# Ten masks on ScalarE in every second head, and an earlier register read on TensorE

## What is computed

```python
for h in range(8):
    Wx = x @ Ws[h] + Wb[h]
    s = Wx[dst] @ a_w[h, :d] + Wx[src] @ a_w[h, d:] + a_b[h]
    s = leaky_relu(s, 0.2)
    alpha = segment_softmax(s, dst)
    out[h] = segment_sum(alpha * Wx[src], dst)
```

## Time and profile before

| | |
|---|---|
| Runs | 561.11, 562.78 and 562.98 us, median 562.78 |
| The profiled execution | 560.58 us, of which the span from its first to its last instruction is 558.8 |
| Start and tables | 0 to 21.5 us |
| Counting of edges | 21.5 to 147.8 us |
| Masks and weighted sums of the eight heads | 147.9 to 261.4 us |
| The rest | 261.4 to 558.8 us |
| Busy share of the span | PE 89%, DVE 85%, ACT 61%, POOL 12% |

### The profile page before, as it was taken

The page is one execution under the profiler, slowest core; times in us unless marked ns, Lnnn a source line. Parts: engine busy times, 40 slices in busy tenths (PEclk is TensorE's granted clock), DMA queues, the critical chain, the costliest instruction groups (busy, mean ns, idle before and its releaser), DMA issues.

```text
span 558.8 us, 12125 instructions
## 1 busy us (share of the span) xinstructions
PE 499.0 (89%) x4635; PEld 371.2 (66%) x4636; DVE 472.7 (85%) x933; ACT 342.7 (61%) x663; POOL 68.3 (12%) x83
## 2 busy tenths in 40 slices
PE   1879999887589999999889999998999999999995
PEld 1757777765488888889777754543456686877662
DVE  7899999799899999996898947997687686997771
ACT  5365555567889999997456452334444457865830
POOL 3000000000000000000000020122423520321232
PEclk9989999999989999999999989999999999999999
DMA  6980000002001111100000039100001017966111
GB/s 173 360 290 2 1 2 1 2 4 95 3 1 50 54 74 60 54 3 2 1 0 2 1 112 392 43 1 1 2 11 50 38 64 261 389 242 220 61 53 52
DMA packets 25306, 45.14 MB, mean 81 GB/s; under 512 B 6961, under 2 KB 7205, under 8 KB 25248
## 3 DMA queue, kind: packets, MB, share of 16 engines
q1 hardware_dynamic: 23264, 39.16, 20.4%
q0 software_dynamic: 1952, 5.18, 2.5%
q10 hardware_dynamic: 32, 0.01, 0.0%
HBM read 33.23 MB, written 11.95 MB: 81 GB/s over the span
## 4 chain that ended last, share of the span: by engine, by line
DVE 41%; PE 37%; issue 10%; DMA 5%; ACT 4%; POOL 3%; ACTq 0%; POOLq 0%; DVEq 0%
PE bank L1390 7%; PE bank L1414 5%; PE bank L1457 4%; DVE work L1082 4%; DVE big L950 4%; PE bank L1780 4%; PE bank L1464 4%; PE bank L1561 3%; PE bank L1574 2%; DMA aux<-xperm_scratch 2%; DVE st L849 2%; PE bank L1368 2%; POOL row L489 2%; DVE rings L1082 2%; DMA out<-aux 2%
## 5 line engine op out<-in xcount | busy, mean ns | idle before, releaser
L950 DVE TENSOR_TENSOR big<-mid 128x1536 f16<-128x1536 f16 (+1 forms) x100 | 92.1, 978 | 0.0
L1457 PE MATMUL bank<-big 128*128 128x160 f16 x552 | 72.2, 248 | 4.1 <-DVE big L950 4.1
L1561 PE MATMUL bank<-big,work 128*128 128x130 f16 x1080 | 67.2, 224 | 8.4 <-DVE work L1082 8.4
L1561 PEld LDWEIGHTS bank<-big,work 128*128 128x128 f16 x1080 | 64.0, 100 | 10.5 <-DVE work L1082 4.9
L1457 PEld LDWEIGHTS bank<-big 128*128 128x128 f16 x552 | 51.7, 111 | 6.7 <-DVE big L950 6.3
L657 ACT ACTIVATE mid<-aux,small 128x1280 f16<-128x1280 f32 x36 | 47.4, 1349 | 0.7 <-DVE work L1082 0.4
L1574 PE MATMUL bank<-big,mid 128*128 128x260 f16 x400 | 47.1, 275 | 0.1
L1656 PE MATMUL bank<-mid 128*128 128x512 f16 x200 | 47.2, 378 | 0.0
L556 ACT ACTIVATE big<-bank 128x160 f32 x92 | 27.9, 304 | 26.5 <-PE bank L1464 25.2
L556 ACT ACTIVATE mid<-bank 128x160 f32 x92 | 27.8, 303 | 25.8 <-PE bank L1464 24.4
L1574 PEld LDWEIGHTS bank<-big,mid 128*128 128x128 f16 x400 | 38.2, 96 | 7.5 <-issue 0.3
(11 more groups left out here) (313 smaller groups left out, 1123.4 us busy)
## 6 DMA issues: line engine op xcount, KB each, us to landing
big<-in_L_ffn_W SPq DMA_DIRECT2D x10, 1024.0 KB, 14.0
mid<-in_L_ffn_W SPq DMA_DIRECT2D x6, 1024.0 KB, 15.1
xperm_scratch<-work SPq DMA_DIRECT2D x1, 5753.0 KB, 20.2
aux<-thr_scratch SPq DMA_DIRECT2D x8, 640.0 KB, 3.8
aux<-xperm_scratch SPq DMA_DIRECT2D x8, 523.0 KB, 4.5
row<-in_x SPq DMA_DIRECT2D x1, 2304.0 KB
aux<-in_L_gnn_Ws SPq DMA_DIRECT2D x4, 256.0 KB, 4.5
work<-in_L_gnn_W SPq DMA_DIRECT2D x1, 1024.0 KB, 14.5
```

Of the source, the lines that this page charges most:

```text
L950: return V.tensor_tensor(out.rearrange("p c (v two) -> p c v two", two=2), values.rearrange("p (v two) -> p v two", two=2).unsqueeze(1).to ...
L1457: mm(count_bank(base, k)[:, 0:RW], L_ring[:, slot, k * CH + j, :], R_ring[:, slot, k * CH + j, :], start=j == 0, stop=False)
L1561: ins = mm(acc_region(h, t), weighted[i % NC][:, t * P:(t + 1) * P], VP[:, s, part, h, :, :].rearrange("p b f -> p (b f)"), start=False, s ...
```

## The change

Three edits. BY_ACT becomes a list of pairs (head, tile): in heads 1, 3, 5 and 7 ACT makes all ten masks, in heads 0, 2, 4 and 6 still nine. ACT's copy hi(h + 1) moves from behind the mask of s = 4 to behind that of s = 6. At the start, the four transposes of W0 go to banks 0 to 3 instead of 0, 1, 0, 1; PE waits for the tables, reads the first batch's addresses ahead of w0_T(2) and w0_T(3), and before the first window it waits for two of ACT's four copies instead of four.

```diff
-BY_ACT = (0, 1, 2, 3, 4, 6, 7, 8, 9)
+BY_DVE = 5
+BY_ACT = [(h, s) for h in range(H) for s in range(T) if h % 2 or s != BY_DVE]
...
-                act(W0T[k], bank[k % 2][:, :], ACT.Copy).then_inc(sem("w0T_ready"), 1)
+                act(W0T[k], bank[k][:, :], ACT.Copy).then_inc(sem("w0T_ready"), 1)
...
-            def mask(h, m):
-
-                i = h * len(BY_ACT) + m
+            def mask(h, s):
+
+                i = BY_ACT.index((h, s))
                 if i >= NZ:
-                    h2, m2 = divmod(i - NZ, len(BY_ACT))
-                    a.wait_ge(sem("cz_made"), h2 * T + BY_ACT[m2] + 1)
-                s = BY_ACT[m]
+                    h2, s2 = BY_ACT[i - NZ]
+                    a.wait_ge(sem("cz_made"), h2 * T + s2 + 1)
...
-                for m in range(len(BY_ACT)):
-                    mask(h, m)
-                    if m == 4 and h + 1 < H:
+                for s in range(T):
+                    if (h, s) in BY_ACT:
+                        mask(h, s)
+                    if s == 6 and h + 1 < H:
                         hi(h + 1)
...
-                    if s in BY_ACT:
-                        m = h * len(BY_ACT) + BY_ACT.index(s)
+                    if (h, s) in BY_ACT:
+                        m = BY_ACT.index((h, s))
...
-                if k >= 2:
-                    pe.wait_ge(sem("w0T_ready"), k - 1)
-                transposes(W0[:, k, :, :].rearrange("p h f -> p (h f)"), bank[k % 2], "w0T_psum")
+                transposes(W0[:, k, :, :].rearrange("p h f -> p (h f)"), bank[k], "w0T_psum")
...
+            pe.wait_ge(sem("tables"), 1)
+            pe.wait_ge(sem("lo_table"), 1)
+            at = targets(mybir.EngineType.PE, 0)
             w0_T(2)
             w0_T(3)
-            pe.wait_ge(sem("tables"), 1)
             pe.wait_ge(sem("C_zeroed"), 2)
             pe.wait_ge(sem("pool_ready"), 1)
-            pe.wait_ge(sem("w0T_ready"), K)
-            at = targets(mybir.EngineType.PE, 0)
+            pe.wait_ge(sem("w0T_ready"), 2)
             count(0, 0, 0)
```

## The result

| | before | changed |
|---|---|---|
| median of 20 runs each, us | 561.71 | 559.37 |
| range of the runs, us | 558.37 to 566.62 | 557.12 to 561.06 |
| profiled execution, us | 560.58 | 557.17 |
| its span, us, and mean clock | 558.8, 0.987 | 555.4, 0.990 |

The ratio is 0.9949, with an interval of 0.9928 to 0.9969. The change makes the kernel faster by about 0.5%; the prediction was 561.4 us, no measurable difference likeliest, and a range that ended 0.5 us above what came.

The account below looks back on a forecast made before the run. PE was taken to bound the kernel up to about 104.8 us, then DVE until about 246.7 us. Start 1.05 plus masks 0.3 gave 1.35 us, from 562.8 to 561.4 us; range 559.9 to 562.9 us.

Parts of the forecast that it names:

- The base: Whole kernel: the time before the change, given as 562.8 us, from which the gain is subtracted.
- the masks' give-back: Mask stage: DVE waits 0.63 us for ACT in each pair of heads, against 0.73 us gained.
- the start's clip: Linear layer's start: DVE's first low half limits PE's gain to 1.14 us; 1.05 us taken.
- The allowance for the slow reads: Before the linear layer: PE's last register read, moved among DMAs, leaves 1.0 to 1.14 us; 1.05 taken.
- DVE is held once: Edge counting: DVE waits only at line 999, for 3.6 us, so PE's gains before it go through.
- a wait of 2.5: Sign at line 999: DVE's wait shrinks from 3.6 to 2.5 us, the line starting at about 103.7 us.
- The separate banks in themselves remove no wait: Start: both copies that w0_T(2) and w0_T(3) waited for were done before 18.65 us.
- The masks, 0.3 us foretold: Mask stage: three pairs of heads each gain 0.73 us and give back 0.63, 0.3 us in all.
- The clock: Rival, first batch: PE's clock halves inside windows and products, one group eating the start's gain; 562.5 us, chance 0.07.
- nothing of the start survives: Rival, start: DVE is the true limit from 41 us, or reads take all the gain; 562.5 us, chance 0.12.
- masks overlap less in a row of ten: Rival, mask stage: masks take 1.349 us each and ACT sets the pace; 564.1 us, chance 0.06.
- ACT doesn't hold DVE: Rival: masks give 2.2 us and the start 1.1, so 559.5 us; chance 0.25 with the cases between.

Follow-up runs that it names:

- the third run: The changed kernel, unaltered, measured a third time: 558.75 us, ratio 0.9957 to the kernel before.
- masks-only kernel: Changed kernel with only the masks' edits, the start as in the kernel before: 560.46 us, ratio 0.9972.
- ring of five: Changed kernel with a fifth mask buffer instead of four: 556.31 us, ratio 0.9925 to the kernel before.
- start-only kernel: Changed kernel with only the start's edits, the masks as in the kernel before: 559.60 us, ratio 0.9950.
- banks only: Changed kernel with separate banks and the two-copy wait, but the first register read left behind the transposes: 559.87 us, ratio 0.9976.

## Why the prediction came out wrong

Three terms failed. The base, 562.78 us, was read from three runs and lies 1.1 us above the median of twenty; the masks' give-back was put at 0.63 us a pair and is 0.55; the start's clip was put at 1.05 us and is 1.26. The measured gain is 2.34 us where 1.35 was foretold: 0.44 of the difference are the two terms of the sum, and 0.55 are the clock and what stays open. It was the base that put the time outside the range, which hangs on 562.8: shifted by 1.1 us it would be 558.8 to 561.8.

**The start, 1.05 us foretold, 1.26 measured.** Each step up to the clip held: the removed wait, the read under the fillers, the first window at 19.80 (19.7 foretold), the clip by DVE's first low half. The size was off in "It gains only where it waited for ACT, 0.81 us": DVE's shift was 0.92 (40.10 to 39.18), since the instruction of line 1018 now starts 0.08 us before the end of the one ahead of it, where behind the wait nothing overlapped. PE's shift at the linear layer was 1.19 us; it grew to 1.23 at line 1000 and 1.26 at the join, more than the bound of 1.14, and what adds the last 0.07 no run shows. The allowance for the slow reads, which pulled 1.14 down to 1.05, wasn't needed: with reads of 1.86 and 1.90 us the third run had the same join, if with nothing to spare. It was worked out from the last read alone, and the two ahead of it count as well.

"DVE is held once" misread the stage. DVE also waits at 95.59 and 98.50 us, so its lead at line 999 is no slack of 3.6 us that PE's gain uses up; the wait was 3.55 or 3.56 us in every trace of every kernel, and the sign "a wait of 2.5" didn't come. That changed no term of the sum. That the fall of the clock behind the fp32 products "costs nothing now" held: the masks-only kernel had no fall there, and its join was at 147.83, before at 147.86.

**The banks.** "The separate banks in themselves remove no wait" is right of the waits of w0_T(2) and w0_T(3) and misleads about the whole: the wait that cost was that for all four copies, and with two banks the first windows, which use banks 0 and 1, have to wait for copies 2 and 3. The prediction counted it as removed; it did not see that, with the short wait, the read would have been hidden without being moved. That changed no number.

**The masks, 0.3 us foretold, 0.53 measured.** The mechanism, the heads and the place (tile 2 of heads 2, 4 and 6) were right. The give-back of 0.63 us a pair was too large: it measured 0.73 - 0.53 / 3 = 0.55. Two products lie 1.26 us apart at the wait (206.02 and 207.28) instead of 0.74; of the difference 0.43 is shown as idle, and the rest is the overlap that a wait takes away. Every small term of the path had been set high: masks came every 1.2525 us rather than 1.254, hi took 1.20 rather than 1.22, and a freed buffer was taken up after 0.85 rather than 0.91. With these the prediction's own sum is 0.85 + 12.525 + 1.20 + 1.45 = 16.03, which against DVE's 15.49 is a wait of 0.54. The term is a difference between two paths of 16 us: 0.5% of either is nearly half of what a pair gains. Two slips of the text changed little: 237.74 to 238.95 is 1.21 us and not 1.22, and by the prediction's own terms the whole change turns slower from 1.30 us a mask, not 1.31.

**The sum.** So 1.35 us should have been 1.79. One term was short by a sixth and the other by nearly a half, both in the same direction. The prediction took 1.7 us as about what a measurement can tell from none; the right sum lies just above it.

**The base.** The prediction took 562.78 us, the median of three runs, as what the change is subtracted from. Twenty runs have 561.71 and all 108 a median of 561.95. Of the 2.0 us between the predicted and the measured time, 1.1 are this.

**The clock.** As a rival it was given 0.07 and one sign. It occurs in single executions of both kernels, costs or spares them 1 to 3 us, and adds about 0.5 us in the changed kernel's favour over all runs, which the kernel before run again shows to be within what happens to one and the same program. Between the 2.27 us at equal clock and the 1.79 us traced, 0.5 +- 0.4 us stays open, and where it arises no run here shows. It isn't seen behind the masks: from 261 us (line 1574) to the end the two traces of the kernel before take 297.3 and 295.8 us, the three of the changed kernel 295.7, 298.6 and 297.1.

**The other rivals.** That nothing of the start survives, and that masks overlap less in a row of ten, are excluded, by the join at 146.60 and by 1.2525 us for each of ten masks. "ACT doesn't hold DVE" is not true of the changed kernel, but it is of the ring of five: 1.38 + 2.16 = 3.54 us are gained in its trace ahead of the products over all edges (join at 146.48, line 1575 at 257.93), close to this rival's 3.3, beside 5.3 us in the times. What is above 3.5 is open in the same way as above; there are only six runs of it.

## What to carry to other kernels

Where one engine makes what another uses up through a ring, write the path around the ring as a sum of spacings and count buffers before moving work: here one more buffer was worth 1.6 us, three times the 0.53 that the moved masks gave without it. A wait placed for the last of several copies holds everything behind it, register reads included; shorten the wait to what the next use needs before reordering anything. And for a difference of half a per cent, take the base from many runs and the size from landmarks in the trace: three traces of one kernel put the join at 146.60, 147.93 and 146.58 us, the odd one being a fall of the clock.

## What the runs showed of the hardware

The granted clock fell to half in the stretch of the fp32 products at 24.8 us in one execution of the changed kernel, with PE busy without a gap in every microsecond from 20 us on. In two executions of the kernel before it fell at 22.9 us, 2.4 us after PE had gone to work again, and at 28.4; in the first and the third trace of the changed kernel not before 148 us. It stayed down for 3.5 to 17 us. The later falls cost nothing where PE had time to spare (from 29.9 to 33.4 us in the start-only kernel). A read of a register from a tensor took 0.54 to 0.61 us with quiet DMAs, 0.76 to 0.79 while inputs were loaded, and mostly 0.9 to 2.0 beside the 5.75 MB of zeros being written, in both places where that transfer ran. PE's sequencer made such a read 2 us before the weights of transposes that stand ahead of it in the program were loaded (16.8 and 18.86 us, banks only).
